# Attention ahead of a mixture of experts: packed 16-bit query rows turned by DMA, and the expert weights loaded from ScalarE's queue

## The reference, cut to what matters

```python
def attention(query, key, value, key_abundance, ...):        # 2 x 1024 tokens, 256 wide; 64 keys; 16 heads of 16
    q = query @ w_q.T + b_q;  k = key @ w_k.T + b_k;  v = value @ w_v.T + b_v
    scores = einsum('bhqd,bhkd->bhqk', q, k) * scale + log(key_abundance)[:, None, None, :]
    attn = softmax(scores, axis=-1)
    return einsum('bhqk,bhkd->bhqd', attn, v) (heads side by side) @ out_proj_weight.T + out_proj_bias

def ffn(x, gate_w, expert_bias, w1, w2, w3):                  # 8 experts, hidden 704, the 2 best for each token
    scores = softmax(x @ gate_w.T);  sel = top_k(scores + expert_bias, 2)
    tokens sorted by expert; routed = x[token] * score
    h = silu(routed @ w1[e]) * (routed @ w3[e]);  out[token] += h @ w2[e]

x = x + attention(layernorm(x), ctx, ctx, abundance, ...)
x = x + ffn(layernorm(x), ...)
```

## Time and profile before

| | us |
|---|---|
| median of 3 runs | 453.25 (452.56 to 455.9) |
| profiled execution, its time | 454.74 |
| profiled execution, its span | 453.0 |

### The profile page before, as it was taken

One profiled execution on the slowest core, in us unless ns is written; L12 is line 12 of the kernel. 1 busy time (PEld: TensorE's weight loads), 2 busy tenths in 40 slices (PEclk: granted clock), 3 DMA queues, 4 the chain that ended last, 5 costly groups with the idle time before them and its releaser, 6 DMA issues.

```text
span 453.0 us, 10327 instructions
## 1 busy us (share of the span) xinstructions
PE 363.5 (80%) x2657; PEld 270.0 (60%) x2658; DVE 261.2 (58%) x635; ACT 195.2 (43%) x352; POOL 232.8 (51%) x281
## 2 busy tenths in 40 slices
PE   3468998999997872113999999999999999999830
PEld 2435777877785761111667677776676777777620
DVE  2888765666766128891655555555555555556400
ACT  4265668575756524301433333344443333333300
POOL 6566665444345347504245556555556555554330
PEclk9798999999999655555999999999999999999995
DMA  6912552332337344102467778777777777888636
GB/s 186 362 62 66 174 168 74 112 122 81 122 112 218 95 150 144 30 1 71 98 121 139 135 134 136 133 135 134 135 140 134 131 138 135 134 134 136 99 56 197
DMA packets 106677, 57.55 MB, mean 127 GB/s; under 512 B 82581, under 2 KB 101282, under 8 KB 106626
## 3 DMA queue, kind: packets, MB, share of 16 engines
q1 hardware_dynamic: 98848, 46.78, 41.3%
q0 software_dynamic: 7488, 10.39, 15.5%
q10 hardware_dynamic: 322, 0.15, 0.1%
HBM read 28.62 MB, written 11.60 MB: 89 GB/s over the span
## 4 chain that ended last, share of the span: by engine, by line
PE 69%; DVE 11%; issue 6%; DMA 6%; POOL 2%; ACT 2%; SPq 1%; POOLq 0%; DVEq 0%; ACTq 0%
PE sc L1360 11%; PE sc L1361 10%; PE sc L1362 10%; PE bank L1376 5%; PE bank L1379 5%; PE bank L1245 4%; PE bank L1378 4%; PE bank L1314 4%; PE ptps L1290 3%; DMA acc<-xn,put_now 2%; PE bank L1303 2%; DMA w_hi<-n_L_xattn_in_proj_weight 1%; DMA stage_w<-in_L_ffn_w 1%; DMA arena<-xn 1%; PE sc L1169 1%
## 5 line engine op out<-in xcount | busy, mean ns | idle before, releaser
L1360 PE MATMUL sc<-w_hi,arena 128*128 x312 | 98.6, 316 | 11.8 <-DMA arena<-xn 9.8
L616 POOL DMA_INDIRECT acc<-xn,put_now x39 | 62.5, 1601 | 70.3 <-DVE xn L1128 57.9
L1361 PE MATMUL sc<-w_hi,arena 128*128 x312 | 98.4, 315 | 0.0
L1362 PE MATMUL sc<-w_lo,arena 128*128 x312 | 98.3, 315 | 0.0
L524 POOL TENSOR_TENSOR w_lo<-stage_w,w_hi 128x1408 f16<-128x1408 f32 (+3 forms) x32 | 72.7, 2286 | 44.9 <-ACT w_hi L640 44.9
L1115 DVE SCALAR_TENSOR_TENSOR arena<-sc,slot_score,arena 128x352 f32<-128x352 f32 x78 | 45.5, 584 | 84.8 <-ACT arena L785 84.8
L785 ACT ACTIVATE arena<-sc,slot_score 128x352 f32<-128x352 f32 x78 | 43.1, 553 | 116.6 <-PE sc L1362 115.5
L1376 PE MATMUL bank<-w_hi,arena 128*128 x234 | 63.8, 273 | 3.3 <-DVE xn L1128 1.8
L1379 PE MATMUL bank<-w_lo,arena 128*128 x234 | 61.7, 273 | 0.0
L585 POOL DMA_INDIRECT arena<-table,get_now x39 | 42.1, 1080 | 33.3 <-POOL get_now L582 32.3
L1378 PE MATMUL bank<-w_hi,arena 128*128 x195 | 53.2, 273 | 0.0
(11 more groups left out here) (192 smaller groups left out, 640.1 us busy)
## 6 DMA issues: line engine op xcount, KB each, us to landing
stage_w<-in_L_ffn_w SPq DMA_DIRECT2D x16, 704.0 KB, 4.5
stage_w<-in_L_ffn_w SPq DMA_DIRECT2D x16, 256.0 KB, 3.0
stage_w<-in_L_ffn_w SPq DMA_DIRECT2D x32, 64.0 KB, 2.6
acc<-arena SPq DMA_DIRECT2D x16, 128.0 KB, 1.7
table<-xn SPq DMA_DIRECT2D x16, 128.0 KB, 1.8
arena<-in_x SPq DMA_DIRECT2D x2, 896.0 KB, 7.9
arena<-table,get_now POOLq DMA_INDIRECT x39
arena<-xn SPq DMA_TRANSPOSE x39
```

What stands on the lines that cost most here:

```text
L616: pool.indirect_dma_start(out=acc[:, :], out_offset=bass.IndirectOffsetOnAxis(ap=put_now[par][:, 0:1], axis=0), in_=y_sb[par], in_offset=N ...
L1360: pe.matmul(ps[:, c, :], gT[par][:, k, :], w_hi[:, cols], start=k == 0, stop=False)
L1361: pe.matmul(ps[:, c, :], gT[par][:, KD + k, :], w_hi[:, cols], start=False, stop=False)
L1362: ins = pe.matmul(ps[:, c, :], gT[par][:, k, :], w_lo[:, cols], start=False, stop=k == KD - 1)
```

## The change

Six edits:

1. **Scores in one contraction.** The 128 rows of a contraction now hold, for one pair of heads, four quarters of 32: query high, query low, query high, ones. Against them stand key high, key high, key low, and the bias (its high and low part). One matmul of 128 columns gives the scores of a pair; eight give the tile. The bias is now the key's share of the query bias plus log abundance, made as a row sum on VectorE. `beta`, `key_diag` and the bias matmuls go.
2. **Rows turned by DMA.** Queries are made as rows (tokens on partitions; six matmuls of 256 columns instead of twelve of 128), packed as 16-bit rows `q16` by ScalarE and VectorE, and turned by a DMA transpose on SyncE (`queries_across`, 8 blocks of 128). The normalised token rows are split into `x16` first and turned the same way (`tokens_across`, 4 blocks). TensorE's `x_transpose` goes. The key rows are packed and turned once.
3. **Loads on ScalarE's queue.** All loads of expert weights, and of most of x, are issued by ScalarE (`load`, `load_piece`, `load_rest_of_x`). SyncE keeps the transposes and the stores.
4. **Pieces placed anew** by `plan` and `late`: large and small pieces take turns in their two buffers, and the last four are handled in steps 16 to 19.
5. **The first normalisation's apply** moves from ScalarE to GpSimd from tile 4 on (`rows_apply`), and all of a step's lists are written out; the hardware loop goes.
6. **Preparation reordered**, with fewer constants ahead of the first use, and the maxima of a tile made by one instruction.

The core of the diff:

```diff
-        STEP_HALVES = [(1, 0), (1, 1), (2, 1)] + [(e, 0) for e in range(2, 7)] + [(3, 1), (4, 1)]
-        BESIDE = {4: (5, 1), 14: (6, 1)}
+        plan = [[0], [1, 0], [0, 1]] + [[0], [1, 1], [0]] * 4 + [[0], [1, 1]] + [[]] * 3
+        late = [[]] * T + [[0], [0], [1], [1]]
...
+            def load(n):
+
+                act.wait_ge(s["wlo"], rank(n)[1] + 1)
+                act.wait_ge(s["whi"], rank(n)[1] + 1)
+                load_piece(act, n)
...
+                for n in at_step[t][0:1]:
+                    piece_high(n)
+                if here(t, 1):
+                    probs_across(t - 1, 0)
                 if here(t, 2):
-                    bt = tt - 2
+                    bt = t - 2
                     act.wait_ge(s["ot_ps"], bt + 1)
...
                     act.activation(oT[:, :], bk6[:, KD * P:2 * KD * P], ACT.Copy).then_inc(s["ot_sb"], 1)
...
+                for n in at_step[t][1:]:
+                    piece_high(n)
                 if here(t, 1):
...
+                    probs_across(t - 1, 1)
+                if t + 1 < STEPS:
+                    for n in at_step[t + 1] + late_step[t + 1]:
+                        load(n)
+                if late_step[t]:
+                    act.wait_ge(s["pt_ps"], 2 * T)
+                for n in late_step[t]:
+                    piece_high(n)
```

```diff
-            def scores_half(par, c):
-
-                o = sc_ps[par][:, c * HS:(c + 1) * HS]
-                cc = slice(c * P, (c + 1) * P)
-                pe.matmul(o, qT_hi[par][:, cc], kb_hi[:, c, par, :], start=True, stop=False)
-                pe.matmul(o, qT_hi[par][:, cc], kb_lo[:, c, par, :], start=False, stop=False)
-                pe.matmul(o, qT_lo[par][:, cc], kb_hi[:, c, par, :], start=False, stop=False)
-                return pe.matmul(o, ones16[:, :], beta[:, par, c * HS:(c + 1) * HS], start=False, stop=True)
...
+                    for c in range(H // 2):
+                        ins = pe.matmul(sc_ps[t % 2][:, c * P:(c + 1) * P], qT[t % 2][:, c, :], kb[:, t % 2, c, :],
+                                        start=True, stop=True)
+                    ins.then_inc(s["s_ps"], 1)
```

```diff
+            def tokens_across(tt):
+
+                sp.wait_ge(s["xh_lo"], tt + 1)
+                if tt >= 2:
+                    sp.wait_ge(s["q_ps"], tt - 1)
+                sp.dma_start_transpose(xT[tt % 2], x16[tt % 2]).then_inc(xt_in[tt % 2], 16)
+
+            def queries_across(tt):
+
+                sp.wait_ge(s["q16_hi"], tt + 1)
+                sp.wait_ge(s["q16_lo"], tt + 1)
+                if tt >= 2:
+                    sp.wait_ge(s["s_ps"], tt - 1)
+                sp.dma_start_transpose(qT[tt % 2], q16[tt % 2]).then_inc(qt_in[tt % 2], 16)
...
+            def step(t):
+
+                if here(t, -2):
+                    queries_across(t + 2)
```

More of the change, by code:

```diff
@@ L236, in xattn_moe @@
         ht_in = [s["ht_in0"], s["ht_in1"]]
+        xt_in = [s["xt_in0"], s["xt_in1"]]
+        qt_in = [s["qt_in0"], s["qt_in1"]]
         def landed(j, par):
             return 16 * ((j - par) // 2 + 1) if isinstance(j, int) else 8 * (j - par) + 16
[L242 to L249, removed]
-            with eng.Fori(3, UT - 1) as u:
-                step(u, 0, None)
-                step(u, 1, None)
-            for t in range(T - 2, T + 4):
-                step(t // 2, t % 2, t)
@@ new lines, in xattn_moe, with add_piece @@
+        STEPS = T + 4
+        FIRST_X = LN_GROUPS[1][1]
+        plan = [[0], [1, 0], [0, 1]] + [[0], [1, 1], [0]] * 4 + [[0], [1, 1]] + [[]] * 3
+        late = [[]] * T + [[0], [0], [1], [1]]
+        halves = [iter([(e, g) for e in range(E) for g in range(2)]) for _ in range(2)]
+        placed = [0, 0]
+        PIECES = []
+        def add_piece(kind):
+            PIECES.append((*next(halves[kind]), kind, placed[kind] % 2))
+            placed[kind] += 1
+            return len(PIECES) - 1
@@ L410, in _ @@
-            attention_steps(sp, step)
-            for n in range(LATE + 2, len(PIECES)):
-                load(n)
+            def tokens_across(tt):
[9 more added lines that the diff above has]
+                sp.dma_start_transpose(qT[tt % 2], q16[tt % 2]).then_inc(qt_in[tt % 2], 16)
@@ L414, in _ @@
+            for t in range(STEPS):
+                step(t)
             sp.wait_ge(s["scores_in"], 2)
@@ L898, in _ @@
+            tokens_low(2)
+            queries_low(0)
+            for tt in range(*LN_GROUPS[2]):
+                first_stats(tt)
+            first_moments(*LN_GROUPS[2])
+            queries_low(1)
+            dve.wait_ge(s["kt_in"], 16)
+            spread_keys(0)
+            tokens_low(3)
+            spread_keys(1)
             n_r = [0]
@@ L1214, in _, with values @@
             across(pt_ps2, wo_n, "woT_ps")
-            pe.wait_ge(s["wvT_sb"], 1)
-            for b in range(B):
+            def values(b):
                 for k in range(KD):
@@ L1315, in step, with probs_over @@
                     pe.matmul(o, shares16[:, :], bo16[:, :], start=False, stop=True).then_inc(s["attn_ps"], 1)
-            attention_steps(pe, step)
+                if here(t, 1):
+                    probs_over(t - 1, 1)
+            def probs_over(bt, c):
+                if bt >= 1:
+                    pe.wait_ge(s["pt_sb"], 2 * bt)
+                else:
+                    pe.wait_ge(s["v_sb"], 4 * B)
+                    pe.wait_ge(s["woT_sb"], 1)
+                for q in range(4):
+                    j = 4 * c + q
+                    ins = pe.transpose(pt_ps2[:, j * P:(j + 1) * P], prob[bt % 2][:, j * P:(j + 1) * P], idt)
+                ins.then_inc(s["pt_ps"], 1)
+            for t in range(STEPS):
+                step(t)
             pe.wait_ge(s["selected"], 2)
```

761 lines of the change are left out of this document (349 added, 412 removed).

## The result

The changed kernel takes 481.2 us (median of 4 runs, 479.1 to 483.56), the one before 454.57 in the same sessions. The ratio is 1.059, 95% interval 1.051 to 1.067: 6% slower. The forecast was 463, with a range to 478: right in direction, and too small by 18 us.

A forecast was written before the change was run, and what follows sets the result against it. TensorE was taken to bound attention now, and after the change a loop through each load's landing on ScalarE's queue. +4.4 (start) + 15.1 (13 steps) - 10.0 (tail) = +9.5 us, so 463, range 444 to 478.

The forecast's parts named there:

- The mechanism: Attention steps: ScalarE's load issue, landing 5.07 and 4.02 us of work form one loop; large step 9.09, small 7.2.
- A: Attention: landing is short (4.2 us) and the clock holds, mean step 7.88, whole 446 us; chance 0.15.
- B: Attention: ScalarE runs ahead, landing hides in TensorE's shadow, TensorE bounds a step at 6.05, whole 420 us; chance 0.10.
- D: Whole kernel: change is neutral, steps of 8.3 us, preparation gains 0 to 2, whole 450 to 456; chance 0.22.
- I charge it to one step in three: 0.5.: Attention: low clock after TensorE's stand adds 1.6 us on the loop, charged as 0.5 a step; bounds 0 and 3.
- The bound of 3: Attention: upper bound, in us a step, on the low clock's charge, which was taken as 0.5.
- C: Attention: low clock throughout, TensorE's work about 11 us a step, whole 489; chance 0.10 with what lies between (over 475).
- The start: Preparation and steps 0 to 2: three landings show, exponential of tile 2 at 52.5 against 48.11, +4.4 us; bounds -3, +9.
- The tail: Exponential of tile 15 to last choice of experts: spread low halves and shorter routing steps, -10.0 us; bounds -4, -16.
- the 9.9 put on them: Tail: VectorE routing steps stretched beside GpSimd's low halves, 4.5 us from two steps and 5.4 from four more.
- The covers: Attention: hidden work and transposes (landing in 2.55 us) have most of a step's slack; failure adds up to 2.5.
- The range: Whole kernel: 444 to 478 us, covering bounds of landing and tail, leaving out B and most of C.

The follow-up runs named there:

- the experiment with the filler alone: Changed kernel plus 22 unused TensorE matmuls of 256 columns before the turned attention output in large-piece steps 3 to 15, loads unmoved; 472.31 us.
- second version: From first version: first token rows' transposes ahead of rest of x and loads 2, 3; later loads behind query's transpose; exponential 0 ahead of query copy 3; 439.67 us.
- the experiment: Kernel before the change, without low halves of the last expert's four pieces, GpSimd filling zeros after the choice of experts; one run, 449.01 us.
- first version: Changed kernel with loads on SyncE a step ahead, first loads and rest of x ahead of transposes, two pieces made early; 451.95 us.

## Why the prediction was right and wrong

**The mechanism was right.** The loop through issue, landing, piece, probabilities, output copy, projection and turned blocks is the chain of the profile. Its prices at full clock were right too. Over the nine large steps from 59.24 to 187.87 the mean from issue to the piece is 5.07 us, the value taken; from the piece to the next issue the one step at full clock (113.72 to 117.68) took 3.96, against 4.02. The small step at full clock (129.25 to 136.66) took 7.41, against 7.2. Rivals A, B and D fell with it. B's bound for TensorE, 6.05, was near (6.24), but the order kept it out of reach, as argued.

**The step that failed is the clock.** "I charge it to one step in three: 0.5." Eight of the nine large steps ran the projection and the turned blocks at or near the low level; from the piece to the next issue took 5.22 on average, 1.26 more than 3.96. The four small steps took 9.01, 1.6 more than 7.41; their second stand had no term at all. Together 9 x 1.26 + 4 x 1.6 = 17.7 us, or 1.36 a step and not 0.5: 11 us too little. (Each price at full clock is one step's; the experiment with the filler alone shows 9 us.) The rest of the 14.5 us is small: 2.4 from four issues ahead of the exponential of tile 15, 0.6 from nine large steps in 13 instead of two in three, 0.3 from the two full-clock prices. The error of thought: a fall at 147 us in the kernel before, in one place, was counted as rare. But the loop makes the same stand in every large step, so its price had to be charged to each; eight of nine paid it. The bound of 3 held the truth; the value didn't follow from the rows. The Trainium skill, "TensorE: Matmul & The Clock Gate", section "HAM oscillation", described it: bursts between waits, each starting low. The large steps agree with it (0.50 behind stands of 2.2 to 3.9 us in eight of nine); the falls behind stands of 0.3 and 1.0 us are not of that pattern. The result lies in the band over 475 that had a chance of 0.10 with C; C's own form, low all through and TensorE the bound at 11 us a step, did not come.

**The start was mis-sized and misnamed.** The forecast was +4.4 for three landings that show; it was +11.6, and taking every such landing away brought 2.6 us. The exponential of tile 0 was forecast at 37.4 and came at 41.00. It was ready long before: scores of tile 0 start at 26.37 (26.88 before) and VectorE's subtraction starts at 28.28 and takes 1.22. What failed is the step that followed ScalarE's list by the waits on loads alone and left out GpSimd (four low halves in a row, 9.04 us, ahead of the token rows of tile 5) and the query copies behind five pieces:

```profile
35.74 1.38 ACT L629 ACTIVATE w_hi<-stage_w 128x1408 f16<-128x1408 f32 x1 [2.95 <-DMA stage_w<-in_L_ffn_w]
...
37.14 0.60 ACT L668 ACTIVATE arena<-bank 128x512 f16<-128x512 f32 x1
```

```profile
38.34 0.37 PE L1165 MATMUL bank<-arena 128*128 128x256 f16 x1 [10.70 <-DVE arena L866]
```

TensorE stood still 10.7 us for that copy, and its clock was 0.50 from there to 59 us, so two more steps were long too (7.3 of the 11.6 us lie ahead of the exponential of tile 0, which came at 33.73 before). Only the second version, which takes all the covers away at once, brought it forward.

**The tail was right** in sum, -10.7 against -10.0, in part by luck. Its parts: 8.13 us from the exponential of tile 15 to the weighted values, against 7.4. The 256 wide step and the 96 wide one were put at 0.5 together; the first took 0.42, the second stayed at 1.69 beside other low halves. The price of the low halves by themselves is 7.7 in the experiment, against the 9.9 put on them.

**The covers held.** Transposes land in 4.4 and 4.8 us and not in the 2.55 taken, but TensorE waits for none of them between 59 and 190 us.

**The range** took in the bounds of landing and tail and not the clock's own, 3 us a step, which over 13 steps is 2.5 x 13 = 32 us more than the value taken. It was cut where C began, though no row made the prices between rare.

## What to carry to other kernels

A load belongs on a queue and at a place where nothing in the loop stands between its issue and its use: here a step's lead was worth at least 18 us of 100, and freeing the computing engine's queue another 7 to 12; without the lead, the other queue made it worse. When one stand of the kernel is followed by a low clock, charge that to every repetition of the stand in a loop, and look for further stands, short ones too. If removing one of two things ahead of an instruction changes nothing, look in the trace for the other before naming a third.

## What the hardware showed

- Issuing can take much longer when two queues issue at once. Two 64 KB loads took 3.01 us on ScalarE's queue while a transpose took 2.89 on SyncE's. But in the changed kernel (100.21 to 102.36) the same two queues overlapped too, at 1.15 and 1.20. The Trainium skill, "Perfetto Trace Analysis", section "DMA Instruction — HWDGE (DVE, Sync)", describes a block that makes descriptors, is shared by VectorE's and SyncE's queues and is locked by one issuer at a time. The first case would agree with such a lock between ScalarE and SyncE, the second does not show it; the cause stays open.
- Without the loads the transposes land sooner: 3.1 and 2.4 us instead of 4.4 and 4.8. That transposes slow the loads was not tested; the large loads landed in 4.2 us before and in 4.7 after.
- A stand of 2.05 us ahead of the projection (to 115.91) left the clock at 1.00; one of 2.38 us (to 97.10) was followed by 0.50 until 100.7. Shorter ones went both ways too: 0.31 us (to 92.32, second version) was followed by 0.50, and 1.16 us (to 116.96, same kernel) was not. So a stand comes ahead of each fall that was read here, and its length alone does not tell whether the clock falls.
- A VectorE step that makes a 16-bit low part of 256 columns takes 0.41 us, and 2.92 beside GpSimd's low half of a piece; it ended 0.3 us behind it. The two rows are of the first version at the start:

```profile
34.84 2.92 DVE L867 TENSOR_TENSOR x<-xn,x 128x256 f16<-128x256 f32 x1
```

```profile
34.63 2.85 POOL L530 TENSOR_TENSOR w_lo<-stage_w,w_hi 128x1408 f16<-128x1408 f32 x1 [3.71 <-ACT w_hi L652]
```
